# A graph-network kernel on one Trainium2 core: another table for TensorE's register loads in the stage that counts edge pairs

## The reference

```python
agg = jax.ops.segment_sum(x[src] * norm[:, None], dst, num_segments=n)
```

## Time and profile before

| what | us |
|---|---|
| median of three runs | 5088.47 |
| lowest and highest run | 5082.26 and 5090.49 |
| the profiled execution's own time | 5087.5 |
| its span, first to last instruction | 5086.2 |
| of this, the items' matmuls (line 1457) | 680.6 to 954.7 |

### The profile page before, as it was taken

How to read it: one execution, slowest core, us unless ns; L and a number is a source line. 1 busy time by engine, 2 the same in 40 slices (tenths; PEclk the granted TensorE clock), 3 DMA queues, 4 the chain that set the end, 5 groups by cost and what they waited for, 6 DMA issues and landing times. The chain is left out here.

```text
span 5086.2 us, 60811 instructions
## 1 busy us (share of the span) xinstructions
PE 3733.6 (73%) x16870; PEld 2409.4 (47%) x16871; DVE 2487.1 (49%) x3877; ACT 966.3 (19%) x2688; POOL 2036.5 (40%) x2254
## 2 busy tenths in 40 slices
PE   5977856598999959999988677676667544444459
PEld 2544522256555525555554465565555433433345
DVE  7989977505888871112325644344436522222221
ACT  2937746423000031111221000000001000000011
POOL 0000000102777701011000577777772777777731
PEclk7978979899999979999988855555558755555569
DMA  0000023525888807356344422222225322222215
GB/s 18 0 0 0 0 91 142 211 91 185 295 294 292 296 24 237 124 191 223 132 149 154 169 52 53 53 53 53 53 53 191 124 53 53 53 53 52 53 55 166
DMA packets 162006, 576.87 MB, mean 113 GB/s; under 512 B 44321, under 2 KB 56194, under 8 KB 161613
## 3 DMA queue, kind: packets, MB, share of 16 engines
q0 software_dynamic: 97200, 308.78, 19.8%
q1 hardware_dynamic: 64278, 265.76, 14.7%
q10 hardware_dynamic: 390, 0.60, 0.0%
HBM read 443.46 MB, written 131.51 MB: 113 GB/s over the span
## 5 line engine op out<-in xcount | busy, mean ns | idle before, releaser
L2140 PE MATMUL ps_sum_rgcn<-gathered_rgcn,select_sum_rgcn 128*128 x3328 | 998.9, 449 | 683.0 <-DMA gathered_rgcn<-by_dst,row 370.9
L2140 PEld LDWEIGHTS ps_sum_rgcn<-gathered_rgcn,select_sum_rgcn 128*128 128x128 f32 x3328 | 779.1, 314 | 759.2 <-issue 754.6
L2055 POOL DMA_INDIRECT gathered_rgcn<-by_dst,row x782 | 741.5, 948 | 238.2 <-issue 230.9
L2055 POOL DMA_INDIRECT gathered_rgcn<-by_src,row x686 | 647.6, 944 | 245.3 <-issue 200.4
L718 PE MATMUL ps_sum_arma<-gathered_sum_arma,select_sum_arma 128*128 128x384 f32 x1664 | 551.0, 491 | 19.3 <-DMA gathered_sum_arma<-arma,other 16.2
L704 POOL DMA_INDIRECT gathered_sum_arma<-arma,other x416 | 393.7, 946 | 377.9 <-POOLq L790 211.4
L1650 PE MATMUL ps_sum_arma<-pair_counts_sum_arma,parts_sum_arma 128*128 128x448 f16 x2625 | 519.4, 354 | 5.1 <-DMA pair_counts_sum_arma<-pairs 5.1
L2209 DVE TENSOR_TENSOR select_sum_rgcn<-one_hot_sum_rgcn,ps_coef_sum_rgcn 128x2048 f32<-128x2048 bf16 x52 | 119.0, 2288 | 680.6 <-PE ps_sum_rgcn L2140 680.5
L718 PEld LDWEIGHTS ps_sum_arma<-gathered_sum_arma,select_sum_arma 128*128 128x128 f32 x1664 | 308.2, 190 | 262.0 <-issue 65.5
L752 DVE TENSOR_TENSOR acc_arma_end<-acc_arma_end,ps_sum_arma 128x768 f32 x416 | 396.8, 954 | 55.6 <-PE ps_sum_arma L718 34.3
L2173 ACT COPY sums_sum_rgcn<-ps_sum_rgcn 128x128 f32<-128x128 f32 x100 | 26.6, 266 | 1868.3 <-PE ps_sum_rgcn L2140 1868.3
(11 more groups left out here) (444 smaller groups left out, 5202.1 us busy)
## 6 DMA issues: line engine op xcount, KB each, us to landing
pair_counts_sum_arma<-pairs SPq DMA_DIRECT2D x125, 800.0 KB, 4.4
by_src<-rows_rgcn_src_table SPq DMA_DIRECT2D x50, 576.0 KB, 2.8
by_dst<-rows_rgcn_dst_table SPq DMA_DIRECT2D x50, 576.0 KB, 3.8
exact<-whole_pairs SPq DMA_DIRECT2D x25, 800.0 KB, 3.4
pairs<-whole_pairs POOLq DMA_DIRECT2D x25, 800.0 KB, 5.1
pair_counts_sum_x<-pairs SPq DMA_DIRECT2D x25, 800.0 KB, 4.4
pair_counts_sum_gcn<-pairs SPq DMA_DIRECT2D x25, 800.0 KB, 4.3
air_counts_sum_neighbour<-pairs SPq DMA_DIRECT2D x25, 800.0 KB, 4.3
```

The costliest lines, as they stand in the source:

```text
L2055: nc.gpsimd.indirect_dma_start(got[:, n % PLACES, :], None, table, bass.IndirectOffsetOnAxis(ap=o.row[:, n % C:n % C + 1], axis=0)).then_i ...
L2140: nc.tensor.matmul(ps[:, bass.ds(slot, P)], select[:, parity, u, :], rows[:, bass.ds(place, D)], start=False, stop=False, skip_group_check ...
```

## The change

The list gets another layout, and the loop another rhythm.

- `q.item_at` holds 2-byte unsigned integers, in rows of 16 (32 bytes). A row serves 12 items: 12 bank columns, then 3 thresholds, and one unused place.
- A threshold stands for four items, and is that of the fourth of them, whose block is the latest.
- TensorE loads 15 registers for 12 items, so 48 loads instead of 72.
- The wait for `freed`, with the `nop` that carries it, is done once for four items, together with the wait for `made`. The matmuls of the other three items have no wait in front.
- The loop's body is 96 items, run 6 times, instead of 32 items, run 18 times.

```diff
+FOUR = 4
+DOZEN = 3 * FOUR
+ROW = 16
...
-            nc.vector.tensor_scalar(items[:, :, 1], b_at[:, :], 1.0, None, ALU.add)
+            nc.vector.tensor_scalar(q.item_at[:, :, DOZEN:DOZEN + DOZEN // FOUR],
+                                    b_at[:, :].rearrange("p (n h a) -> p n h a", h=DOZEN // FOUR, a=FOUR)[:, :, :, FOUR - 1],
+                                    1.0, None, ALU.add)
...
-            nc.vector.tensor_scalar(items[:, :, 0], tile_at[:, :], float(SPAN), None, ALU.mult)
+            nc.vector.tensor_scalar(q.item_at[:, :, 0:DOZEN], tile_at[:, :].rearrange("p (n a) -> p n a", a=DOZEN),
+                                    float(SPAN), None, ALU.mult)
...
-            with pe.Fori(0, ITEMS // V // 2) as i:
-                for u in range(2 * V):
-                    if u % 8 == 0:
-                        table = load(PE, q.item_at, i * (4 * V) + 2 * u, 16, (SPANS - 1) * SPAN)
-                    if u % 4 == 0:
-                        pe.wait_ge(made, i * (2 * V) + u + 4)
-                    pe.wait_ge(freed, table[u % 8 * 2 + 1])
-                    nc.tensor.nop(nofuse=True)
-                    nc.tensor.matmul(ps[:, bass.ds(table[u % 8 * 2], SPAN)], source[:, u // V, u % V // 2, :, u % 2],
+            BODY = 2 * DOZEN * V // FOUR
+            with pe.Fori(0, ITEMS // BODY) as i:
+                for u in range(BODY):
+                    if u % DOZEN == 0:
+                        table = load(PE, item_at, i * (BODY // DOZEN * ROW) + u // DOZEN * ROW, DOZEN + DOZEN // FOUR,
+                                     (SPANS - 1) * SPAN)
+                    if u % FOUR == 0:
+
+                        pe.wait_ge(made, i * BODY + u + FOUR)
+                        pe.wait_ge(freed, table[DOZEN + u % DOZEN // FOUR])
+                        nc.tensor.nop(nofuse=True)
+                    nc.tensor.matmul(ps[:, bass.ds(table[u % DOZEN], SPAN)], source[:, u // V % 2, u % V // 2, :, u % 2],
                                      target[:, u % V, :], start=False, stop=False, skip_group_check=True).then_inc(multiplied, 1)
...
-        q.item_at = c.sb("item_at", [P, 2 * ITEMS], I32)
+        q.item_at = c.sb("item_at", [P, ITEMS // DOZEN, ROW], U16)
```

More of the change, by code:

```diff
@@ L1277, in staircase_stage @@
         chunk_at = sb("chunk_at", [P, ITEMS])
-        items = q.item_at[:, :].rearrange("p (n a) -> p n a", a=2)
         ps = c.psum("ps", [P, 8, 512])
@@ L1418, in pair_counts_stage @@
         stored, kept = (stored0, stored1), k.kept
+        item_at = q.item_at[:, :, :].rearrange("p n a -> p (n a)")
         block = c.block()
```

## The result

| kernel | median us | lowest to highest | runs |
|---|---|---|---|
| before | 5088.3 | 5082.26 to 5090.49 | 4 |
| changed | 5147.12 | 5141.3 to 5149.56 | 4 |

What follows compares the result with a forecast made beforehand. TensorE's sequencer, above all its 72 register loads, was taken to bound the 274 us stage. With VectorE taking over at 214 or 215 us, 5087.5 - 59 = 5028.5 for the execution, 5029 forecast; range 5016 to 5130 us.

Steps and rivals of the forecast that it cites:

- The load: TensorE's register load of 15 2-byte numbers, not shown by any row; claimed between 0.59 and 3.6 us.
- the most likely case: VectorE takes over the stage for any load up to about 1.5 us; a gain of 59 or 60 us, chance 0.48.
- Outside the load: TensorE's stream between loads: 12 items cost 2.25 us besides the load, with 9 of 12 waits taken out.
- the five prices worked out: TensorE's load: 0.59 by bytes, 1.04 by registers, 1.5 four-register steps, 1.95 16-byte steps, 3.3 to 3.6 no step.
- The stretch: TensorE's loads lengthened, by transfers in the author's reading: 34 us before; 34 to 60 in the slow rival.
- The rival of fifteen registers alone: No fast step for 2-byte numbers in TensorE's sequencer: load 3.3 to 3.6 us, 28 to 69 us slower, chance 0.24.
- L = 2.7: Load time in us above which TensorE's stream, 48 x (2.25 + L) + 2 + 34, exceeds the stage's 274 us.
- The waits: Four items in the matmul loop wait for the fourth one's bank, earlier by at most some items' time; cost 0.
- What becomes late next: The stage's next limit: VectorE's 204.4 us plus 10, so 214 or 215, for any load up to about 1.5 us.
- the case's own range: Program time if VectorE takes over: 5018 (VectorE at its best, 192 + 10) to 5040 (226) us.
- The lower clock: Rival: a lower clock of TensorE in this stage, chance 0.03.

Runs made afterwards that it cites:

- after_stores_late: Changed kernel with both transfers of every row of counts put off until all rows are done; items took 277 us, program 5678.78 us, one run.
- u16_16: Changed kernel, 2-byte list, loading all 16 numbers of a row instead of 15; 5618.39 us, ratio 1.0125 to the kernel before.
- before_u16: Kernel before with only the list's width changed to 2-byte integers; 5768.19 us, ratio 1.039 to the kernel before.
- i32_rows_of_17: Changed kernel with 4-byte integers, 15 registers per load, in rows of 17 numbers (68 bytes); items took 305 us, program 5609.59 us, one run.
- before_one_wait: Kernel before with the wait for a free bank done once for four items; 5543.35 us, ratio 0.9943 to the kernel before.
- i32_15: Changed kernel with the list in 4-byte integers, 15 registers for 12 items; 5498.31 us, ratio 0.9896 to the kernel before.
- i32_16: Changed kernel with 4-byte integers, loading all 16 numbers of a row; 5470.85 us, ratio 0.9852 to the kernel before.
- i32_20: Changed kernel with 4-byte integers in rows of 20 for 16 items, 36 loads; 5503.86 us, ratio 0.9858 to the kernel before.
- after_exact_late: Changed kernel with only SyncE's queue's transfers put off until all rows are done; items took 295 us, program 5654.78 us, one run.

## Why the prediction was wrong

The mechanism and the terms were there; the step that failed is "The load": the most likely case took up to 1.5 us for 15 registers of 2 bytes, and they took 3.551 us, so that the loads, which were to be hidden behind VectorE, became 170 us of TensorE's stream, with 53 us of stretch on top.

- *Outside the load*: right. 2.25 us for 12 items was counted. after_stores_late gives (277 - 2) / 48 - 3.55 = 2.18.
- *The load*: wrong. Of the five prices worked out, 0.59, 1.04, 1.5, 1.95 and 3.3 to 3.6 us, it was the last: 3.551, fifteen alone. The rows that the text had named as the sign for it, a fast load only for 4-byte numbers at aligned addresses, weighed more than I gave them. Against it I had only that the step seemed to be one of 16 bytes, whatever the width. It is not: sixteen 2-byte numbers in 32 bytes get none (3.785 us in u16_16, 3.784 in before_u16). The case had 0.24. Why a 2-byte number gets no step stays open; the runs show only that it costs what a single unaligned number costs (3.551 / 15 = 0.237 us against 3.565 / 15 = 0.238 in i32_rows_of_17).
- *The stretch*: right as a reading. The rival had 34 to 60 us; it is 53.
- *The rival of fifteen registers alone* is what happened. Its sum, with the load and the stretch as measured, is 48 x (2.25 + 3.55) + 2 + 53 = 333 against 330 measured, and its 5116 to 5157 holds 5147. The range given ended at 5130, in the middle of it. The point from which it decides, L = 2.7, was well passed.
- *The waits*: cost 0 was right; no wait shows between the loads in before_one_wait. Taken alone, the merged wait saves 36 us instead of 43, for the stretch grows beside it.
- *What becomes late next*: wrong for the load of 1.5 us, right for one of 1.1. The prediction's own stream for L = 1.5 is 182 us and 34 of stretch, 216, which is above VectorE's 204.4, and yet the text let VectorE take over up to there. i32_15 with 1.57 us took 224 us at TensorE's pace. With 1.1 us (i32_16) VectorE takes over at 198 us busy, and the stage is 195 to 199 us, not 215. A slip besides: a stage of 192 + 10 us gives 5016, where the case's own range begins at 5018.
- *The balance*: outside the loads 48 x 2.2 = 106 us instead of 72 x 2.17 + 5 = 161, so 55 gained. The loads are 48 x 3.55 = 170 instead of 72 x 1.10 = 79, so 91 lost. The stretch is 53 instead of 34, 19 lost. In all 55 us of the 56, and the trace's own sums say the same (273.7 and 328.7 us).
- *The lower clock*, 0.03 of the forecast: no run shows that term, the array itself as the limit of the whole stage. The earlier trace rows has weight loads 0.427 us apart, over four items only. What the runs show is a lower granted clock without longer times between the loads: 160.2 us in sum in before_u16 at 0.54 to 0.67, against 160.6 before at 0.87 to 0.91.

## What to carry to other kernels

By these runs a list that a sequencer reads is laid out for its loads: 4-byte integers (15 took 1.570 us, where 15 of 2 bytes took 3.551), every load from a multiple of 16 bytes (1.573 us against 3.565 for the same 15), and a number of registers that four divides, padded if need be, for one register more saved nearly half a microsecond a load (1.102 for 16). Halving the width of this one more than tripled the load of the same 16 numbers (1.102 to 3.784 us, before_u16). Where a price hangs on a fast path that only one type has ever shown, the forecast should rest on the slow path until a row shows otherwise. And a gap named after a semaphore should be held against the start of the wait behind it: if the wait found all there, look for the sequencer's own work just before. Adding up all loads and the times between them turns this from one example into an account of the whole stage, and shows how near the next limit is.

## What the runs showed of the hardware

- A register load of 4-byte numbers takes 0.589 us for 8, 1.102 for 16, 1.359 for 20, 1.617 for 24 at aligned addresses; 15 take 1.570, more than 16 (before, i32_20, i32_15). Of 2-byte numbers 15 take 3.551 and 16 take 3.785, from aligned addresses too (after, u16_16). 15 of 4 bytes from an unaligned address take 3.57 (i32_rows_of_17). Aligned means a multiple of 16 bytes from the start of the list.
- The transfers of 800 KB out of SBUF beside the register loads stretch them: loads of 3.55 us go up to 4.85 with GpSimd's transfers (after_exact_late) and up to 6.3 with both (after), and are 3.74 at most without any (after_stores_late).
- The granted clock of TensorE in this stage, in slices of 40 us, was 0.96 to 1.00 in i32_16 (0.91 to 1.00 in its second run), 0.87 to 0.91 in the kernel before, 0.71 to 0.87 in the changed one and 0.54 to 0.67 in before_u16: in these four the lower, the longer the same 576 matmuls took (195, 274, 330 and 493 us). No cost of it shows in the changed kernel or in before_u16: the times between the loads add up to 105.8 us, as in after_stores_late at 0.83 to 0.88 (105.7), and to 160.2, as before (160.6).
